# Experts in pairs of token tiles: the hidden layer of the first two tiles computed turned, weights stationary

## What is computed

```python
xn = layernorm(x)                                   # 2 x 1024 x 512
idx, w = route(xn)                                  # 6 of 32 experts for each token
for w1, w2, g in experts:                           # w1 256 x 512, w2 512 x 256
    h = square(relu(xf @ w1.T)) @ w2.T              # xf: 2048 x 512
    acc = acc + g[:, None] * h
out = x + attention(xn) + acc + shared_expert(xn)
```

## Time and profile before

| | us |
|---|---|
| median of 3 runs (1524.73 to 1525.66) | 1525.64 |
| the profiled execution | 1526.73 |
| its span, first to last instruction | 1525.0 |
| PE busy in the span | 1509.9 (99%) |
| DVE busy | 1132.8 (74%) |
| ACT busy | 837.9 (55%) |

### The profile page before, as it was taken

How to read it: one execution, slowest core, us unless ns; L and a number is a source line. 1 busy time by engine, 2 the same in 40 slices (tenths; PEclk the granted TensorE clock), 3 DMA queues, 4 the chain that set the end, 5 groups by cost and what they waited for, 6 DMA issues and landing times.

```text
span 1525.0 us, 31150 instructions
## 1 busy us (share of the span) xinstructions
PE 1509.9 (99%) x8552; PEld 1302.1 (85%) x8553; DVE 1132.8 (74%) x2586; ACT 837.9 (55%) x1753; POOL 298.3 (20%) x540
## 2 busy tenths in 40 slices
PE   9998999999999999999999999999999999999998
PEld 8877998899899888888888888888888888888886
DVE  7896666666666669859949948967975994994896
ACT  5574666666666635535625635644553553553553
POOL 0003344334344311011002002102102101200211
PEclk9999999999999999999999999999999999999999
DMA  8874777777876612102102103422211210210111
GB/s 318 301 302 165 218 243 233 229 234 228 258 234 207 228 35 70 43 21 76 55 7 79 45 28 120 149 62 85 67 34 41 69 41 21 76 34 28 56 42 55
DMA packets 64774, 184.34 MB, mean 121 GB/s; under 512 B 7136, under 2 KB 7264, under 8 KB 60000
## 3 DMA queue, kind: packets, MB, share of 16 engines
q1 hardware_dynamic: 39888, 112.56, 21.1%
q0 software_dynamic: 16640, 54.54, 13.1%
q10 hardware_dynamic: 8208, 16.78, 2.8%
HBM read 123.29 MB, written 60.56 MB: 121 GB/s over the span
## 4 chain that ended last, share of the span: by engine, by line
PE 96%; DVE 2%; DMA 1%; issue 0%; ACT 0%; ACTq 0%; DVEq 0%; SPq 0%
PE bank L663 8%; PE bank L665 8%; PE bank L993 8%; PE bank L664 8%; PE ps_s L663 7%; PE ps_s L665 7%; PE ps_s L664 7%; PE ps_s L980 5%; PE ps_s L982 5%; PE ps_s L981 4%; PE ps_s L860 4%; PE ps_s L883 4%; PE ps_s L864 3%; PE ps_s L861 3%; PE ps_s L887 3%; PE ps_s L884 3%
## 5 line engine op out<-in xcount | busy, mean ns | idle before, releaser
L1322 ACT ACTIVATE probs<-probs,negmax 128x128 f32<-128x128 f32 (+7 forms) x256 | 197.4, 774 | 122.5 <-DVE negmax L1736 121.9
L1330 ACT ACTIVATE pT_hi<-bank 128x512 fp32r<-128x512 f32 x288 | 164.5, 595 | 143.4 <-PE bank L993 117.5
L1347 DVE TENSOR_TENSOR pT_lo<-bank,pT_hi 128x512 fp32r<-128x512 f32 x288 | 189.7, 684 | 41.0 <-ACT pT_hi L1330 40.0
L1736 DVE CUSTOM_DVE_ANT_0 probs<-ps_s,causal 128x128 f32<-128x128 f32 (+7 forms) x256 | 189.5, 753 | 17.1 <-PE ps_s L982 14.9
L427 POOL TENSOR_TENSOR settled<-ident 128x1 f32<-128x1 f32 x192 | 46.5, 242 | 788.7 <-DVE acc L1765 778.7
L993 PE MATMUL bank<-ident,probs 128*128 128x128 f32 x1152 | 157.0, 272 | 0.0
L993 PEld LDWEIGHTS bank<-ident,probs 128*128 128x128 f32 x1152 | 136.9, 141 | 19.8
L663 PE MATMUL ps_s<-xT_hi,wa_hi 128*128 128x512 f32 x384 | 152.7, 398 | 0.0
L665 PE MATMUL ps_s<-xT_hi,wa_lo 128*128 128x512 f32 x384 | 150.9, 393 | 0.0
L664 PE MATMUL ps_s<-xT_lo,wa_hi 128*128 128x512 f32 x384 | 150.2, 391 | 0.0
L1745 DVE TENSOR_SCALAR probs<-probs,rnorm 128x128 f32<-128x128 f32 (+7 forms) x256 | 133.4, 521 | 9.1
(11 more groups left out here) (197 smaller groups left out, 3596.3 us busy)
## 6 DMA issues: line engine op xcount, KB each, us to landing
eraw<-we SPq DMA_DIRECT2D x37, 1024.0 KB
expert_outputs<-ysb SPq DMA_DIRECT2D x111, 256.0 KB
araw<-wa SPq DMA_DIRECT2D x37, 512.0 KB, 4.3
expert_outputs<-comb ACTq DMA_DIRECT2D x1, 16384.0 KB, 47.4
normed_tokens<-xn SPq DMA_DIRECT2D x4, 1024.0 KB, 10.0
out<-acc SPq DMA_DIRECT2D x16, 256.0 KB
acc<-x SPq DMA_DIRECT2D x2, 1024.0 KB, 13.8
turned_tokens<-xT_hi SPq DMA_DIRECT2D x2, 1024.0 KB, 7.6
```

Of the source, the lines that this page charges most:

```text
L1322: act.activation(pr, pr, ACT.Exp, bias=negmax[:, i % 2, a:a + 1], scale=-1.0, accum_out=rowsum[:, i % 2, a:a + 1]).then_inc(exp_ready, 1)
L1330: act.activation(pT_hi[:, blk % RING, :], ps_t[blk % 2][:, :], ACT.Copy).then_inc(pt_hi_ready, 1)
L1347: dve.tensor_tensor(out_, whole, upper.bitcast(F32), ALU.subtract).then_inc(signal, 1)
L1736: dve.tensor_tensor_reduce(halves(probs[:, i % 2, a, 0:keys]), ps_s[:, s:s + parts, 0:keys // parts], halves(causal[:, SQ - keys:]), -1.0, ...
```

## The change

It touches the experts' stage. The first two tiles of an expert, lo and lo+1, become a pair. `hidden_pair` takes w1 as the stationary operand and the turned tokens of both tiles (256 columns) as the moving one, in two halves m of 12 products; the result is the hidden layer turned already, so these tiles need no `transpose_hidden`. ACT takes relu into `prelu` and the upper part by a second activation, Square; DVE squares and subtracts. `xgT` and `hT` get room for two tiles, `hT` twice; three more PSUM banks are used (`ps_x2`, `ps_p`, `ps_y2`). The tokens of tile lo+1 are turned at the head of the expert instead of behind the previous hidden products. The output of the previous expert's last tile is cut in two: `output_upper` at the head, `output_lower` behind the pair. `output_first` then computes the output of tile lo; tile lo+1's output stands in the loop. ACT and DVE split pieces 0 and 1 of the next weights ahead of the pair's relu, piece 2 between its halves, piece 3 ahead of the loop. The loop runs from lo+2, and the minimum of tiles is three (`LEAST`), which changes the bound MAXT from 160 to 177. DVE gets a wait for the last store (`room_free`) ahead of the first scores of the attention, whose buffers lie over the larger ones. SP's program has no edit.

```diff
@@ -43,7 +43,8 @@
-MAXT = MINT + 2 * E
+LEAST = 3
+MAXT = max(LEAST * (E - n) + min(n * TILES, (T * TOPK + (P - 1) * n) // P) for n in range(E + 1))
...
@@ -217,13 +218,15 @@
-            xgT_hi = sb("xgT_hi", [P, KD, P], F32R, room)
-            xgT_lo = sb("xgT_lo", [P, KD, P], F32R, room)
+            xgT_hi = sb("xgT_hi", [P, KD, 2, P], F32R, room)
+            xgT_lo = sb("xgT_lo", [P, KD, 2, P], F32R, room)
-            hT_hi = sb("hT_hi", [P, KM, P], F32R, room)
-            hT_lo = sb("hT_lo", [P, KM, P], F32R, room)
+            hT_hi = sb("hT_hi", [P, 2, KM, 2, P], F32R, room)
+            hT_lo = sb("hT_lo", [P, 2, KM, 2, P], F32R, room)
+            prelu = sb("prelu", [P, KM, 2 * P], F32, room)
+            phsq = sb("phsq", [P, KM, 2 * P], F32, room)
...
@@ -263,6 +266,9 @@
+        ps_x2 = banks[0][:, :]
+        ps_p = [bank[:, 0:2 * P] for bank in banks[1::2]]
+        ps_y2 = banks[2][:, :]
...
@@ -846,53 +852,85 @@
+            def hidden_pair(lo, s):
+                w_hi, w_lo = w1(hi_slot(s)), w1(lo_slot(s))
+                both = lambda x, k: x[:, k, :, :].rearrange("p t n -> p (t n)")
+                for m in range(KM):
+                    ms = slice(m * P, (m + 1) * P)
+                    if m == 0:
+                        pe.wait_ge(mx_hi, lo + 2)
+                    for k in range(KD):
+                        pe.matmul(ps_p[m], w_hi[:, k, ms], both(xgT_hi, k), start=(k == 0), stop=False)
+                        pe.matmul(ps_p[m], w_lo[:, k, ms], both(xgT_hi, k), start=False, stop=False)
+                    if m == 0:
+                        pe.wait_ge(mx_lo, lo + 2)
+                    for k in range(KD):
+                        mm = pe.matmul(ps_p[m], w_hi[:, k, ms], both(xgT_lo, k), start=False, stop=(k == KD - 1))
+                    mm.then_inc(mh_ready, 1)
+            def output_first(lo, s):
+                w_hi, w_lo = w2(hi_slot(slot_of(s))), w2(lo_slot(slot_of(s)))
+                for m in range(KM):
+                    pe.wait_ge(mhhi_ready, past(lo + (m + 1)))
+                    pe.matmul(ps_y, hT_hi[:, s % 2, m, 0, :], w_hi[:, m, :], start=(m == 0), stop=False)
+                    pe.matmul(ps_y, hT_hi[:, s % 2, m, 0, :], w_lo[:, m, :], start=False, stop=False)
+                    pe.wait_ge(mhlo_ready, past(lo + (m + 1)))
+                    mm = pe.matmul(ps_y, hT_lo[:, s % 2, m, 0, :], w_hi[:, m, :], start=False, stop=(m == KM - 1))
+                mm.then_inc(my_ready, 1)
...
+            def output_upper(p, s, bank):
+                w_hi, w_lo = w2(hi_slot(slot_of(s))), w2(lo_slot(slot_of(s)))
                 pe.wait_ge(mhhi_ready, past(p + 1))
                 for m in range(KM):
-                    pe.matmul(ps_y, hT_hi[:, m, :], w_hi[:, m, :], start=(m == 0), stop=False)
-                    pe.matmul(ps_y, hT_hi[:, m, :], w_lo[:, m, :], start=False, stop=False)
+                    pe.matmul(bank, hT_hi[:, s % 2, m, 1, :], w_hi[:, m, :], start=(m == 0), stop=False)
+                    pe.matmul(bank, hT_hi[:, s % 2, m, 1, :], w_lo[:, m, :], start=False, stop=False)
+            def output_lower(p, s, bank):
+                w_hi = w2(hi_slot(slot_of(s)))
                 pe.wait_ge(mhlo_ready, past(p + 1))
                 for m in range(KM):
-                    mm = pe.matmul(ps_y, hT_lo[:, m, :], w_hi[:, m, :], start=False, stop=(m == KM - 1))
+                    mm = pe.matmul(bank, hT_lo[:, s % 2, m, 1, :], w_hi[:, m, :], start=False, stop=(m == KM - 1))
                 mm.then_inc(my_ready, 1)
...
             def expert_tiles(e, s, lo, hi, es):
-                pe.wait_ge(ew_lo, (e + NSH) * WP + 2)
-                hidden_tile(lo, slot_of(s))
-                after = pair_bound(pe, e + 2)
+                turn_tokens(lo + 1, ps_x2)
                 if s:
-                    output_tile(lo - 1, slot_of(s - 1))
+                    output_upper(lo - 1, s - 1, ps_y2)
                 else:
                     with pe.If(es > 0):
-                        output_tile(lo - 1, slot_of(SLOTS - 1))
-                transpose_hidden(lo, (e + (NSH + 1)) * WP)
-                with pe.Fori(lo + 1, hi) as p:
+                        output_upper(lo - 1, SLOTS - 1, ps_y2)
+                after = pair_bound(pe, e + 2)
+                pe.wait_ge(ew_lo, (e + NSH) * WP + 2)
+                hidden_pair(lo, slot_of(s))
+                pe.sem_inc(mt_ready, 2)
+                turn_tokens(lo + 2, ps_x)
+                if s:
+                    output_lower(lo - 1, s - 1, ps_y2)
+                else:
+                    with pe.If(es > 0):
+                        output_lower(lo - 1, SLOTS - 1, ps_y2)
+                pe.wait_ge(ew_lo, (e + (NSH + 1)) * WP)
+                output_first(lo, s)
+                with pe.Fori(lo + 2, hi) as p:
                     hidden_tile(p, slot_of(s))
-                    output_tile(p - 1, slot_of(s))
+                    pe.wait_ge(y_copied, past(p - 1))
+                    output_upper(p - 1, s, ps_y)
                     transpose_hidden(p)
+                    output_lower(p - 1, s, ps_y)
                 return after
             over_experts(pe, expert_tiles)
             last = pair_bound(pe, E)
-            output_tile(last - 1, slot_of(SLOTS - 1))
+            output_upper(last - 1, SLOTS - 1, ps_y2)
+            output_lower(last - 1, SLOTS - 1, ps_y2)
...
@@ -1240,15 +1291,27 @@
+            def relu_pair(lo, m):
+                act.wait_ge(mh_ready, lo + (m + 1))
+                act.wait_ge(mhsq_ready, past(lo))
+                act.activation(prelu[:, m, :], ps_p[m], ACT.Relu).then_inc(mrelu_ready, 1)
+            def upper_pair(lo, m, s):
+                act.wait_ge(mrelu_ready, past(lo + (m + 1)))
+                act.activation(hT_hi[:, s % 2, m, :, :].rearrange("p t n -> p (t n)"), prelu[:, m, :],
+                               ACT.Square).then_inc(mhhi_ready, 1)
...
             def expert_uppers(e, s, lo, hi, es):
                 arrived, slot = e // 2 + (NSH // 2 + 2), slot_of(s + 2)
-                relu_hidden(lo)
-                upper_tokens(lo + 1)
+                upper_tokens(lo + 1, 1)
                 upper_weights(0, slot, arrived)
+                after = pair_bound(act, e + 2)
+                upper_weights(1, slot, arrived)
+                relu_pair(lo, 0)
+                upper_pair(lo, 0, s)
+                upper_weights(2, slot, arrived)
+                relu_pair(lo, 1)
+                upper_pair(lo, 1, s)
+                upper_tokens(lo + 2)
                 if s:
-                    copy_output(lo - 1)
+                    copy_output(lo - 1, ps_y2)
                 else:
                     with act.If(es > 0):
-                        copy_output(lo - 1)
-                upper_hidden(lo)
-                after = pair_bound(act, e + 2)
-                upper_weights(1, slot, arrived)
-                with act.Fori(lo + 1, hi) as p:
+                        copy_output(lo - 1, ps_y2)
+                copy_output(lo, ps_y)
+                upper_weights(3, slot, arrived)
+                with act.Fori(lo + 2, hi) as p:
                     relu_hidden(p)
                     upper_tokens(p + 1)
-                    copy_output(p - 1)
-                    upper_hidden(p)
-                upper_weights(2, slot, arrived)
-                upper_weights(3, slot, arrived)
+                    upper_hidden(p, s)
+                    copy_output(p - 1, ps_y)
                 return after
             over_experts(act, expert_uppers)
-            copy_output(pair_bound(act, E) - 1)
+            copy_output(pair_bound(act, E) - 1, ps_y2)
...
@@ -1487,7 +1554,7 @@
-                chain(dve.tensor_scalar(pairs_f, pairs_f, 2.0, None, ALU.max))
+                chain(dve.tensor_scalar(pairs_f, pairs_f, float(LEAST), None, ALU.max))
...
@@ -1643,18 +1710,33 @@
+            def square_pair(lo, m):
+                dve.wait_ge(mrelu_ready, past(lo + (m + 1)))
+                dve.tensor_tensor(phsq[:, m, :], prelu[:, m, :], prelu[:, m, :], ALU.mult).then_inc(mhsq_ready, 1)
+            def lower_pair(lo, m, s):
+                dve.wait_ge(mhhi_ready, past(lo + (m + 1)))
+                dve.wait_ge(mhsq_ready, past(lo + (m + 1)))
+                subtract(hT_lo[:, s % 2, m, :, :].rearrange("p t n -> p (t n)"), phsq[:, m, :],
+                         hT_hi[:, s % 2, m, :, :].rearrange("p t n -> p (t n)"), mhlo_ready)
...
             def expert_lowers(e, s, lo, hi, es):
                 slot = slot_of(s + 2)
-                square_hidden(lo)
-                lower_tokens(lo + 1)
+                lower_tokens(lo + 1, 1)
                 lower_weights(e + 2, 0, slot)
-                lower_hidden(lo)
                 after = pair_bound(dve, e + 2)
                 lower_weights(e + 2, 1, slot)
-                with dve.Fori(lo + 1, hi) as p:
+                square_pair(lo, 0)
+                lower_pair(lo, 0, s)
+                lower_weights(e + 2, 2, slot)
```

(43 more changed lines are left out.)

30 lines of the change are left out of this document (10 added, 20 removed).

## The result

| | before | after |
|---|---|---|
| median of 4 runs, us | 1525.18 | 1556.88 |
| lowest to highest, us | 1523.57 to 1525.66 | 1553.27 to 1562.15 |
| profiled execution, us (its span) | 1526.73 (1525.0) | 1553.27 (1551.5) |

The change makes the kernel slower: the ratio is 1.0212, with a 95% interval of 1.0182 to 1.0243. The profiled execution of after is the fastest of its four, so its trace shows a loss of 26.5 us, not of 31.7.

The account below looks back on a forecast made before the run. PE was taken to bound the experts. Removed products -12.8, late loads +44, first expert +2.0 and list +0.8 gave +34 us on 1525.6: 1560 us, range 1526 to 1585.

Parts of the forecast that it names:

- S: The moment of an expert's first instruction, from which the prediction counted its times in us.
- the rival with the hidden load: Raw-weight loads land within 4.6 us of issue, so the 44 us are not lost: 1515.6 us, chance 0.12.
- Which loads are late: Loads issued in three-tile experts among experts 1 to 30 arrive late, 19 in all; none behind four tiles.
- How late: A raw-weights load takes 7.1 us from issue, ends 5.5 and 8.2, arriving 4.4 us after the expert's start.
- The chain from arrival to output: From raw weights' arrival through ACT, DVE and PE, the first tile's output ends 4.45 us later.
- the cover: PE has other work until 6.57 us into the expert, so weights arriving up to 2.1 us cost nothing.
- The gain: Products removed from PE: a three-tile expert takes 10.20 us against 10.59, saving 12.8 us over 32 experts.
- The pair's head: Second tile's tokens at the pair's start: ready about S + 1.35, wanted by PE at S + 1.40; costed at nothing.
- The first expert: Its raw weights arrive at 142.19 and hold up the first pair: +2.0 us, from 0 to 4.
- The clock as a rival: PE's waits in late experts drop its clock to 1.2 GHz in every second one: 1650 us, chance 0.05.
- The list: MAXT from 160 to 177 gives 96 list products 17 more columns: +0.8 us, range 0 to 2.4.
- The zero fill: Fill ahead of the experts grows from 64 to 81 tiles, 47.4 to 60 us, hidden by other work.

Follow-up runs that it names:

- the version with the load one step ahead: Changed kernel, with SP issuing the raw-weights load for expert e+4 ahead of the store of expert e's last tile: 1518.81 us, ratio 0.9954.
- The turn of eight: Changed kernel with SP's load for expert e+4 ahead of expert e's last store, plus eight experts instead of four per outer-loop turn: 1537.24 us, ratio 1.0074.
- the kernel before with the late load: Kernel before, with SP issuing the load for expert e+3 behind the store of expert e's first tile instead of ahead: 1555.92 us, ratio 1.0196.

## Why the prediction was right, point by point

**The bound, the sign and the mechanism: right.** PE bounds the experts, the held output's copy delays the load, and the load's landing delays the first output. The load left at S + 7.8 (forecast 7.7). With the load early, in two ways, the loss is gone. What is left is a gain of 4.4 and 5.8 us, about half of the 10 that the rival with the hidden load had forecast (1515.6); the points on the gain and on the back edge below say where the rest is.

**Which loads are late: nearly right.** 18 waits, forecast 19, and all of them in experts behind one of three tiles. The missing one is expert 10's, whose load was there within 5.0 us. ACT waited 2.2 us on average, forecast 3.

**How late: too much.** From issue to arrival the 18 took 4.9 to 7.8 us, with a mean of 6.5, and I had taken 7.1. The arrival R after the expert's start is 3.5 on average, forecast 4.4. The load of the earlier trace rows from which I took the upper side was issued when PE never stood. That a PE that waits asks for fewer gathers would fit, and was not tested.

**The chain from arrival to output: too short.** In the expert above, the third tile's hidden products start at 192.41, which is R + 5.3, and I had R + 4.6 (4.45 and the loop's entry). Two pieces of lower weights take 1.50 and not 1.29, and the last lower half starts 0.48 behind DVE's own square. Undisturbed, those products start at S + 6.9 (190.08 with an expert start at 183.15, in the version with the load one step ahead), and I had 6.7. So the cover is about 1.7 and not 2.1, and a late load costs 3.5 - 1.7 = 1.8 us, forecast 2.3. Over 18 that is 32 us, forecast 44. Compared expert by expert with the version whose load is one step ahead, the late ones have lost 32 us together: it agrees.

**The gain: right in kind, a little too large.** The best undisturbed experts of three tiles take 10.14 to 10.27, forecast 10.20, but the mean is 10.38, and 10.32 in the version whose load is one step ahead (fourteen experts; the fifteenth took 11.11). There the stretch from the first expert to the first projection is 3.7 us shorter than before, with 2.8 lost at the first expert and 4.4 at the back edges, which makes the gain 10.9, forecast 12.8.

**The pair's head: not quite free.** I had costed it at nothing. In five of the late experts PE stands 0.2 to 0.4 us there, 1.6 in all, and the pair starts at S + 1.8 to 2.0 instead of S + 1.4 (184.94 in the expert above). What it waits for there no view shows.

**The first expert: right within its range, for another reason in part.** It takes 19.30 instead of 16.74, so +2.6, forecast +2.0. The windows of after show the clock there:

```profile
140.00:142.00 2.00, 1.33 (x11) 1.34 (x12) 0.61 (x2) 0.00 (x0) 0.00 (x0) 1.00 0.99 412
142.00:144.00 2.00, 2.00 (x12) 1.68 (x10) 0.69 (x1) 1.39 (x3) 0.00 (x0) 0.56 1.00 408
144.00:146.00 2.00, 1.34 (x4) 0.77 (x4) 1.78 (x4) 1.94 (x6) 0.98 (x3) 0.50 1.06 438
146.00:148.00 2.00, 2.00 (x5) 1.26 (x6) 1.64 (x4) 0.32 (x1) 1.15 (x1) 0.50 0.83 322
```

Behind waits of 0.69 and 2.06 us PE worked at 1.2 GHz from 142 to 148.9, while in the kernel before the clock stayed at 1.00 there.

**The clock as a rival: wrong in size, not in kind.** I gave it nine late experts and some 90 us. It fell in one of 18, in the expert with the longest wait of ACT (4.18): PE stood 2.23, and then

```profile
268.00:269.50 1.50, 1.30 (x3) 0.75 (x4) 1.40 (x5) 1.47 (x5) 0.05 (x1) 0.67 0.46 106
269.50:272.00 2.50, 2.50 (x9) 1.85 (x8) 1.33 (x3) 1.19 (x4) 0.00 (x0) 0.51 0.39 146
```

which is 3 us of work at half speed, some 1.5 us lost. The Trainium skill (TensorE: Matmul & The Clock Gate, HAM oscillation — how this bites in real kernels) describes a kernel that loses the clock in every round of its loop, behind waits for DMA longer than any wait of PE in the changed kernel. The turn of eight agrees with it: PE stood over 4 us three times, and the clock fell each time. The prediction took it to hold for waits of 0.5 to 1.2 us, and over all the experts of the changed kernel the clock was 0.99. Waits of 1.81 to 2.56 us brought four falls in the kernel before with the late load.

**The back edge: missed.** Every fourth expert costs 0.3 to 0.9 us more than its like, 4.4 us in seven of them; before, it was 0.05. The sum had no term for it. That the back edge is its place is shown by the turn of eight; why it costs more with the held output at the loop's head is not.

**The list: a cost of 0.8 forecast, a gain measured.** What it costs ahead of the experts can't be told: over the traces the first expert starts anywhere from 134.2 to 137.8. The 2.7 us that the attention is shorter by come with it, and the sum had no term for them. The zero fill took 59.9 us (20736 KB) and stayed hidden, as forecast.

The new sum for the profiled execution is -10.9 + 32 + 2.6 + 4.4 - 2.7 = +25, and 26.5 were measured. It meets the forecast's +34 only because the other runs of after were 3.3 to 8.9 us slower than the profiled one, and because the missed back edge and the gain that I took too large lie on the other side of the lateness that I took too large. The sign and the mechanism were argued well; the closeness of the number is partly luck.

## What to carry to other kernels

If a change holds one tile's output over into the next round, follow everything that waits for its copy, and above all the loads that share a queue with its store: here a load of 1 MB that left 5 us later turned a gain of 6 us into a loss of 32. A prefetch belongs ahead of the store that may wait, not behind it. And before a loop body is doubled to save a branch, look at the rows of the queue that fetches instructions: a back edge of the longer body cost 4 us, some six times what one of the shorter did.

## What was not expected of the hardware

- The landing of a 1 MB load varied between 4.9 and 7.8 us in one execution with the same issue pattern, and that spread may be why the runs of after lie 9 us apart (1553.27 to 1562.15), where the four of before lie 2 (and 17 later ones 4.4); only one run of after has a trace, so it is not shown.
- Waits of PE of 2.06 and 2.23 us each went ahead of a fall of the clock to 1.2 GHz, for 7 and 3 us, in the changed kernel, and so did waits of 1.81 to 2.56 in the kernel before with the late load; one of 2.3 in the kernel before did not, and in its version with the late load one of 2.29 (at 278) didn't either. What tells them apart stays open.
- The attention, whose code on PE is the same, takes 2.7 us less in every trace with the longer list and a turn of four experts (six of them), and in none of the three without it.
- A load issued from ACT's queue cost 0.3 us per expert in the kernel before, in front of an ACT that was busy only two thirds of the time.
